# Row maxima five pairs ahead, first and second row of maxima placed by TensorE, closing product later, in a Perceiver block on one core

## The reference

```python
def _L0_xattn_ref(q, kv, mem, w_q, w_kv, w_concat):
    ...
    qh = (q @ w_q).reshape(B, L, N_HEAD, D_HEAD).transpose(0, 2, 1, 3)
    kvp = c @ w_kv
    k, v = (kvp[..., :D_HEAD], kvp[..., D_HEAD:])
    attn_score = jnp.einsum('bhid,bjd->bhij', qh, k) / np.sqrt(D_HEAD)
    attn_prob = jax.nn.softmax(attn_score, axis=-1)
    out = jnp.einsum('bhij,bjd->bhid', attn_prob, v)
    out = out.transpose(0, 2, 1, 3).reshape(B, L, D)
    return out @ w_concat
...
x = x + _L0_xattn_ref(_layernorm(x, axis=-1), ctx_1024, ctx_1024, ...)
x = x + _L0_attn_ref(_layernorm(x, axis=-1), ...)    # 16 heads of 64 over 256 tokens
x = x + _L0_ffn_ref(_layernorm(x, axis=-1), ...)     # 16 experts and a shared one
```

## Time and profile before

| | us |
|---|---|
| median of 3 runs | 593.12 |
| the three runs | 593.82, 588.09, 593.12 |
| the profiled execution | 588.77 |
| its span | 587.0 |

### The profile page before, as it was taken

One profiled execution on the slowest core, in us unless ns is written; L12 is line 12 of the kernel. 1 busy time (PEld: TensorE's weight loads), 2 busy tenths in 40 slices (PEclk: granted clock), 3 DMA queues, 4 the chain that ended last, 5 costly groups with the idle time before them and its releaser, 6 DMA issues.

```text
span 587.0 us, 11604 instructions
## 1 busy us (share of the span) xinstructions
PE 540.5 (92%) x4366; PEld 289.4 (49%) x4366; DVE 459.7 (78%) x653; ACT 391.5 (67%) x800; POOL 184.2 (31%) x234
## 2 busy tenths in 40 slices
PE   2778998999999999999999998989999988989996
PEld 0343343333333333333333333467767756968885
DVE  5797987889999999999999998563546468595555
ACT  1325887788888888888888988934566552434431
POOL 6000002202302320232123112612466551277752
PEclk9998999999999999999999999998999999799999
DMA  8952011122222121011111210100321030032101
GB/s 315 231 113 100 9 45 36 33 48 37 39 47 60 23 50 33 17 33 18 33 33 17 54 56 4 56 1 19 101 97 28 11 106 2 1 108 82 55 1 36
DMA packets 38539, 32.09 MB, mean 55 GB/s; under 512 B 22226, under 2 KB 30932, under 8 KB 37460
## 3 DMA queue, kind: packets, MB, share of 16 engines
q1 hardware_dynamic: 38484, 31.35, 20.7%
HBM read 20.78 MB, written 0.52 MB: 36 GB/s over the span
## 4 chain that ended last, share of the span: by engine, by line
PE 44%; DVE 39%; SPq 5%; DMA 4%; issue 3%; ACT 2%; POOL 2%; DVEq 0%
DVE mxp L1382 32%; PE bank L804 8%; PE bank L815 6%; PE pairS L891 6%; PE pairS L1056 5%; PE bank L1074 3%; PE pairS L941 3%; SPq L398 2%; PE bank L968 2%; PE bank L1056 2%; PE bank L954 2%; DMA qparts<-mcols 2%; SPq L433 2%; PE bank L747 2%; DMA ctx<-ctxT 2%
## 5 line engine op out<-in xcount | busy, mean ns | idle before, releaser
L1382 DVE TENSOR_REDUCE mxp<-pairS 128x1 f32<-128x1024 f32 x256 | 308.1, 1222 | 23.7 <-PE pairS L798 22.4
L1171 ACT ACTIVATE Pb<-bank 128x512 f32<-128x512 f32 x500 | 272.1, 598 | 43.9 <-PE bank L804 12.6
L804 PE MATMUL bank<-qparts,kparts 64*128 64x512 f32 x500 | 183.3, 448 | 11.6 <-DMA qparts<-mcols 4.1
L798 PE MATMUL pairS<-kparts,qparts 64*128 64x512 f32 x512 | 184.0, 450 | 5.9 <-DVE mxp L1382 3.3
L815 PE MATMUL bank<-Pb,V 128*32 128x256 f32 x2048 | 159.3, 391 | 1.0 <-ACT accS L1157 1.0
L804 PEld LDWEIGHTS bank<-qparts,kparts 64*128 64x128 f32 x500 | 74.7, 185 | 116.2 <-ACT Pb L1171 57.3
L815 PEld LDWEIGHTS bank<-Pb,V 128*32 128x32 f32 x2048 | 43.0, 108 | 88.2 <-issue 42.0
L798 PEld LDWEIGHTS pairS<-kparts,qparts 64*128 64x128 f32 x512 | 74.8, 185 | 11.4 <-DVE mxp L1382 5.3
L597 POOL CAST mcols<-mneg 128x3 fp32r<-128x3 f32 (+1 forms) x28 | 5.3, 188 | 234.6 <-DVE mneg L1393 234.6
L615 POOL TENSOR_TENSOR Pb<-Pb,srd 128x512 f32<-128x512 f32 x32 | 33.3, 1041 | 49.9 <-DVE srd L1457 49.5
L1452 DVE TENSOR_REDUCE smx<-pairS 128x2 f32<-128x512 f32 x32 | 21.8, 686 | 30.3 <-PE pairS L941 30.2
(11 more groups left out here) (194 smaller groups left out, 735.2 us busy)
## 6 DMA issues: line engine op xcount, KB each, us to landing
ctx<-ctxT SPq DMA_DIRECT2D x4, 2048.0 KB, 10.1
wU<-w_up SPq DMA_DIRECT2D x18, 256.0 KB, 3.0
quarters<-accS SPq DMA_DIRECT2D x45, 64.0 KB, 2.0
wD<-w_down SPq DMA_DIRECT2D x18, 128.0 KB, 2.1
wA<-w_qk SPq DMA_DIRECT2D x8, 256.0 KB, 2.7
qparts<-mcols SPq DMA_DIRECT2D x112, 0.5 KB, 2.0
kparts<-kvh SPq DMA_DIRECT2D x32, 32.0 KB, 1.9
qparts<-qh SPq DMA_DIRECT2D x32, 32.0 KB, 2.0
```

Source lines behind the costliest of these rows:

```text
L798: last = mm(dst[:, i * 512:(i + 1) * 512], qparts[rows, at:at + P], kparts[c // NCH][rows, k:k + 512], start=True, stop=True)
L804: mm(dst[:], kparts[g // NCH][rows, s * P:(s + 1) * P], qparts[rows, g * CW:(g + 1) * CW], start=True, stop=True).then_inc(exp_filled, 1)
L1171: A(PT[:, s % 8, :], src, ACT.Exp, scale=1.0 / np.sqrt(XD)).then_inc(exp_free, 1)
L1382: nc.vector.reduce_max(mxp[:, c % 2 * NBLK + blk, kp:kp + 1], pairS[n % 2][:], AX).then_inc(max_free, 1)
```

## The change

Five edits. LEAD = 5: five pairs of chunk 1 are done in the lead-in in place of four, so every maximum is made two slots earlier in the chunks. BY_DMA begins at 2: chunk 1's rows go by TensorE at slot 30 of chunk 0, and SyncE's `place_rows(1)` is gone. `("rows", 0)` stands two pairs sooner in the lead-in's order. In the last chunk the closing product moves from slot 2 to slot 6 and batch 0's transposes from slot 17 to 19, and the exponentials of the slots (3, 4), (8, 9), (13, 14), (18, 19) and (28, 29) are taken in one instruction over both halves of pairS0. `keep_warm` issues 20 transposes of the identity into ACC at TensorE's start and 8 ahead of `("kv", 0, 0)`.

```diff
@@ -52,7 +52,8 @@
 FOR_EXP, FOR_MAX = slice(0, 64), slice(64, 128)
 
 
-LEAD = NBLK + 1
+
+LEAD = 5
 NPAIR_K = S // 1024
 
 
@@ -79,7 +80,7 @@
 
 
 
-BY_DMA = range(1, 15)
+BY_DMA = range(2, 15)
 
 
 def max_parts(c):
@@ -97,8 +98,7 @@
        ("max", 0, 2, 1), ("ks", 0, 4), ("ks", 0, 5), ("max", 0, 3, 1), ("max", 0, 0, 2), ("ks", 0, 6), ("ks", 0, 7),
        ("max", 0, 1, 2), ("max", 0, 2, 2), ("v", 0, 0), ("max", 0, 3, 2), ("qT", 1, 0), ("max", 0, 0, 3),
        ("v", 0, 1), ("max", 0, 1, 3), ("max", 0, 2, 3), ("xT", 1), ("max", 0, 3, 3), ("qT", 0, 1),
-       ("max", 1, 0, 0), ("max", 1, 0, 1), ("max", 1, 0, 2), ("qT", 1, 1), ("max", 1, 0, 3),
-       ("rows", 0)]
+       ("max", 1, 0, 0), ("max", 1, 0, 1), ("rows", 0), ("max", 1, 0, 2), ("qT", 1, 1), ("max", 1, 0, 3), ("max", 1, 1, 0)]
 LATER = {(0, 11): ("kv", 1, 0), (1, 11): ("v", 1, 0), (2, 11): ("kv", 1, 1), (3, 11): ("v", 1, 1)}
 NCHUNK = B * NCH
 
@@ -119,7 +119,7 @@
 
 AT_ONCE, APART = {3: (0, 1)}, {1: (0,), 3: (1,)}
 SIDES_AT = [APART, AT_ONCE, APART, APART, APART, APART, APART, APART]
-AHEAD_OF = [(c, blk, kp) for c in range(1, NCHUNK) for blk in range(NBLK) for kp in range(NPAIR_K)][NPAIR_K:]
+AHEAD_OF = [(c, blk, kp) for c in range(1, NCHUNK) for blk in range(NBLK) for kp in range(NPAIR_K)][LEAD:]
 
 
 def pair_at(g, s):
@@ -147,7 +147,9 @@
 EXP_TURN, MAX_TURN = turns()
 
 LAST_RING = 5
-CLOSE_AT, MEAN_AT, PARTS_AT = 0, 3, 18
+
+WITH_NEXT = [s for s in range(3, KT - 1, LAST_RING) if s % 8 != 7]
+CLOSE_AT, MEAN_AT, PARTS_AT = 0, 7, 20
 
 
 
@@ -453,7 +455,6 @@
                 row = src[n] if isinstance(n, int) else src[bass.ds(n, 1)].rearrange("o p n -> (o p) n")
                 sp.dma_start(buf[:], row).then_inc(landed, 16)
 
-            place_rows(1)
             place_q(3)
             place_k(0, range(0, 2))
             gather(0)
@@ -841,8 +842,16 @@
                                   wcat[:, k, :], start=(k == 0), stop=(k == KD - 1))
                 last.then_inc(y_ps, 1)
 
+            def keep_warm(times):
+
+                for _ in range(times):
+                    tr(ACC[:, 0:P], ident[:], ident[:])
+
             pe.wait_ge(ident_done, 1)
+            keep_warm(20)
             for what in PRO:
+                if what == ("kv", 0, 0):
+                    keep_warm(8)
                 if what[0] == "max":
                     dst = max_ready(*what[1:])
                     for i in range(2):
@@ -1165,10 +1174,18 @@
                         move_of[what[0]](*what[1:])
                     if s == 5 and g:
                         sums_move(g - 1)
-                    src, quad = filled(("s", g, s)), g * QUADS + s // 4
-                    if s % 4 == 0 and quad >= 2:
+                    last = g == NCHUNK - 1
+                    if last and s - 1 in WITH_NEXT:
+                        continue
+                    both = last and s in WITH_NEXT
+                    src, quad = filled(("s", g, s + both)), g * QUADS + (s + both) // 4
+                    if 0 in (s % 4, (s + both) % 4) and quad >= 2:
                         act.wait_ge(pv_done, quad - 1)
-                    A(PT[:, s % 8, :], src, ACT.Exp, scale=1.0 / np.sqrt(XD)).then_inc(exp_free, 1)
+                    if both:
+                        A(PT[:, s % 8:s % 8 + 2, :], pairS[0][:].rearrange("p (a n) -> p a n", a=2), ACT.Exp,
+                          scale=1.0 / np.sqrt(XD)).then_inc(exp_free, 2)
+                    else:
+                        A(PT[:, s % 8, :], src, ACT.Exp, scale=1.0 / np.sqrt(XD)).then_inc(exp_free, 1)
 
             PJ, SB = [half[0], half[1]], [half[2], half[3]]
 
```

## The result

The changed kernel's median is 586.67 us over 20 executions (581.71 to 594.46), that of the kernel before 591.03 us over 20 executions beside it (586.78 to 596.07). The ratio is 0.9918, with a 95% interval of 0.989 to 0.9945: 0.8% less, within one per cent. The prediction gave that 0.42 and a gain of over one per cent 0.52. The time lies in the forecast range of 580.5 to 590.0, 2.2 us above the 584.5 forecast. The median of 593.12 that stood ahead of the prediction came from three executions; over 20 it is 2.1 us lower.

A forecast was written before the change was run, and what follows sets the result against it. In the chunks TensorE and VectorE both need 1.23 us for two slots, so gains lie in lead-in, chunk starts and last chunk. Terms sum to -5.8 us, 588.77 to 583.0; median put at 584.5, range 580.5 to 590.

The forecast's parts named there:

- Row waits: Starts of chunks 2, 3, 5 and 14: TensorE's waits for columns moved by DMA, 4.11 us, all go; -4.1 us.
- Rows 1 by TensorE: Slot 30 of chunk 0: four transposes between saturated slots cost +0.49 us, bounds 0.3 and 1.1.
- The price of LEAD = 5: Chunks: one more pair on VectorE before the first exponential, so every exponential stands 1.23 us later; +1.23 us.
- Rows 0 sooner and the fifth pair: Before slot 0: VectorE's 0.41 us wait at 47.41 for the rows' copy goes; -0.41 us.
- the clock's dip: Chunk 0: VectorE's 1.12 us stop at 53.51, at granted clock 0.50, shrinks; -0.3 us, bounds 0 and -1.1.
- Warm-up: Lead-in: added transposes bring L748 from 3.59 to 1.92 us; -0.8 us goes on, between 0 and 1.08.
- rival C: Slower by the clock: each lower-clock stretch in the chunks costs about 1.12 us, ten give 594.2 us; chance 0.06.
- The detour: Lead-in: L748's end lets the third context load go sooner, then place_q(1)'s last transfers and chunk 1's first maximum; -0.8 us.
- The last chunk: Closing product behind chunk 14's last group: accumulator copy 1.99 us sooner, the tail with it; -1.8 us, bounds -0.5 and -2.3.
- Merged exponentials: Last chunk: five exponentials of 1024 save the start of an instruction each; -0.1 us, bounds +0.4 and -0.5.
- A: The waits move: clock gain missing or hidden by the DMA queue, part of the rows' waits stays; 585.6 us, chance 0.24.
- B: The lead is only a price: VectorE sets the chunks' pace, waits shrink by 2; no change, 587.5 us, chance 0.12.

The follow-up runs named there:

- dma_rows1: Changed kernel with chunk 1's rows by DMA again, place_rows(1) back in SyncE's queue: median 586.08 against 591.06 us, ratio 0.9932.
- lead4: Changed kernel with LEAD = 4 and four pairs of chunk 1 in the lead-in: median 586.09 against 590.95 us, ratio 0.9902.
- late_parts: Changed kernel with batch 0's transposes at slot 25 of the last chunk in place of 19: median 584.97 against 591.54 us, ratio 0.9914.
- full_warm: Changed kernel with 34 and 18 warm-up transposes in place of 20 and 8: median 584.13 against 591.06 us, ratio 0.9915.
- undo_close: Changed kernel with the closing product back at slot 2 and batch 0's transposes at slot 17: median 584.96 against 591.54 us, ratio 0.9913.
- no_warm: Changed kernel without the 28 added warm-up transposes: median 585.68 against 591.54 us, ratio 0.9956.
- again: The changed kernel once more, with no edit: median 586.95 against 591.06 us, ratio 0.9942.
- late_pool: Changed kernel with transposes at slot 25, 34 and 18 warm-up transposes, GpSimd's two low parts before its last additions: 583.56 against 590.95 us, ratio 0.988.

## Why the forecast was right or wrong, step by step

- **Row waits, -4.1 us: right.** 4.43 us of VectorE's idle time and all of TensorE's waits went. dma_rows1 and lead4 show the two causes named: the queue behind place_rows(1) (3.2 us) and the margin of the longer lead. The forecast gave chunk 3's wait to the margin alone; either of the two takes it away.
- **Rows 1 by TensorE, +0.49: right**, 0.50 at 71.74.
- **The price of LEAD = 5, +1.23: right**: -4.28 at the last reduction, -3.05 at the first exponential behind it.
- **Rows 0 sooner and the fifth pair, -0.41: right.** The bounds of the clock's dip (0 to -1.1) hold too, and the 0.3 taken was 0 in this execution; in late_parts and full_warm, with a clock of 1.00 from 40 to 60, the 1.12 became 0.35.
- **Warm-up, -0.8: wrong in its first step in this pair**, L748 in 1.92 us: it took 3.64. The reason stood in the prediction's rival C, the idle time up to 8.54, but its price was looked for in the chunks and not at L748 itself. L748 also began 0.6 us later (12.06 for 11.48), when its context landed, and so the first maximum of chunk 1 came at 42.23 in place of 42.04. The detour behind that step is borne out by the other profiles: L748's end sets the third context load, 22 us later the last transfers of place_q(1) begin to go out, and the first maximum starts 1.88 us after they are issued where VectorE waits for it. With the change's transposes it came 0.9 us sooner than the 42.04 of before in the mean of seven profiles, and in the profiled pair 0.2 us later. So -0.8 is a fair size for the change and was missing from the pair that the sum was checked on. A faster L748 isn't enough, though: in three of the five profiles with the long warm-up the first maximum was late all the same. And what it wins can be lost to the clock from 40 to 60 us: 315.4 us to the start of the last chunk at 0.91 and 316.3 to 317.1 at 0.66 to 0.83 (undo_close, no_warm, again), 321.5 in late_pool, against 314.1 at 1.00.
- **The last chunk, -1.8: the step that failed**, with +2.6. The copy's 4.08 us behind the first exponential, against 3.6 forecast and 5.56 before, was nearly right. The additions behind it came 2.6 us sooner (8.0 for 10.6): 1.5 by the copy, and 1.1 where the fetch of instructions is missing. The sum took the normalization as 4.7 us wherever it stood, "needed for batch 0's normalization only, which then is used at slot 19". It was not asked who else is at work at its new place. It moved 1.8 us later and GpSimd's additions 2.6 us sooner, from a distance of 2.7 us to an overlap: +3.8 us on the normalization (0.97, 0.98 and 1.82 us on three of its rows), 2.5 us on TensorE's next product. And with the collision out of the way the change was worth +0.2 us (lead4), -0.3 (no_warm) or -1.1 (late_parts), where GpSimd's chain or TensorE's own slots bind instead: -1.8 was too large in any case. The earlier trace rows had one of the two ends, the additions at 371.29; the held product at 359.51 of the kernel before, the sign that this chip has such a hold, was in the trace and not read.
- **Merged exponentials, -0.1: 0**, and the pair (3, 4) does delay the copy, by 0.5 us in undo_close.

Put together: of the -5.8 us forecast, 0.8 fall away with the warm-up, 0.3 with the dip, 0.1 with the merges and 4.4 with the last chunk, and the row waits give 0.3 more: -5.8 + 0.8 + 0.3 + 0.1 + 4.4 - 0.3 = -0.5 us up to the next block, as the profiled pair has it. The timed ratio of 0.9918 is worth 4.8 us (3.2 to 6.5 by its interval), so some 4.3 us of the timed gain are not in the marks of this pair. Their likely places are the lead-in, where the profiled pair caught the changed kernel with the slowest L748 of seven profiles, and the stretch behind 380, where the same instructions spread by 7 us; neither was separated from the spread, and both stay open. That the forecast came near, with one term of 1.8 us of the wrong sign, is partly luck of the size of that spread.

Of the rivals, none happened as told. A and B were nearest in their total, but not in their reason: no wait for rows stayed. C's mechanism, idle time that costs the clock, did occur, at 8.4 and, in the last chunk, at 371 us, once each and not in the saturated chunks from 60 to 356 us.

## What to carry to other kernels

When a small serial chain is moved on VectorE, look at what GpSimd does in the new place, not only at the chain's own length: a step of 0.16 us can last as long as the GpSimd instructions beside it. Put the consumer of such a chain where it has slack before shortening the chain; moving one number (20 to 26) won 3.7 us at the mark where GpSimd's shorter additions, which leave work out, won 2.5. A warm-up has to reach up to the work that it is for. Two marks in one trace say more about a change of half a per cent than two medians do. One profile for each kernel isn't enough where the clock differs from execution to execution: the warm-up looked useless in the profiled pair and not in six others.
